# Sparse graph attention on one core: keys and values copied in one ScalarE operation, the key bias added by GpSimd, heavy batches summed by TensorE, distances first

## What is computed

```python
mask = adj + eye(n)
q = (h @ Wq.T + bq).reshape(n, 8, 32)        # k and v the same way
scores = einsum('nhd,mhd->hnm', q, k) / sqrt(32)
scores = where(mask == 0, -1e9, scores)
attn = softmax(scores, axis=-1)
ctx = einsum('hnm,mhd->nhd', attn, v).reshape(n, 256)
h1 = layer_norm(h + ctx @ Wo.T + bo)
out = layer_norm(h1 + relu(h1 @ W1.T + b1) @ W2.T + b2)
```

## Time and profile before

| | |
|---|---|
| median of three runs | 583.97 us (583.55 to 585.06) |
| profiled execution | 582.23 us |
| its span, first to last instruction | 580.4 us |
| mean granted TensorE clock | 0.952 of full speed |
| HBM traffic | 242 GB/s over the span |

### The profile page before, as it was taken

How to read it: one execution, slowest core, us unless ns; L and a number is a source line. 1 busy time by engine, 2 the same in 40 slices (tenths; PEclk the granted TensorE clock), 3 DMA queues, 4 the chain that set the end, 5 groups by cost and what they waited for, 6 DMA issues and landing times.

```text
span 580.4 us, 7599 instructions
## 1 busy us (share of the span) xinstructions
PE 500.2 (86%) x2434; PEld 399.7 (69%) x2434; DVE 452.5 (78%) x1066; ACT 181.5 (31%) x435; POOL 244.4 (42%) x366
## 2 busy tenths in 40 slices
PE   3999897875899999898898989969868888789994
PEld 2888796765568748755784776569545777469884
DVE  0788889998899999998999998786988998451103
ACT  0121142313432362252226124522522032432340
POOL 6111156433531576555654535414455536304133
PEclk9999999989799999997999999988978899789998
DMA  8999779998988699698769674425657823401011
GB/s 293 417 421 414 260 242 376 417 408 348 330 320 328 234 353 323 224 385 291 251 226 363 232 272 147 180 89 211 229 176 227 300 83 112 125 0 38 1 37 40
DMA packets 39227, 141.08 MB, mean 243 GB/s; under 512 B 4872, under 2 KB 15368, under 8 KB 35088
## 3 DMA queue, kind: packets, MB, share of 16 engines
q1 hardware_dynamic: 24336, 95.16, 43.9%
q0 software_dynamic: 13328, 43.55, 21.8%
q10 hardware_dynamic: 1520, 1.85, 0.9%
HBM read 123.74 MB, written 16.80 MB: 242 GB/s over the span
## 4 chain that ended last, share of the span: by engine, by line
PE 45%; DVE 35%; issue 9%; ACT 4%; DMA 3%; POOL 3%; POOLq 0%; another core or an unknown queue 0%; ACTq 0%; SPq 0%; DVEq 0%
DVE found L497 11%; PE ps L1031 10%; PE ps L1633 7%; PE ps L1044 7%; PE ps L1011 4%; PE ps L999 3%; PE ps L817 3%; PE ps L1651 2%; DVE stats L1098 2%; DMA work<-q_table,row_of 2%; DVE slots L663 2%; DVE slots L595 2%; DVE slots L676 2%; PE ps L818 2%; DVE work L547 1%
## 5 line engine op out<-in xcount | busy, mean ns | idle before, releaser
L497 DVE FIND_INDEX8 found<-ones,adj_buf 128x8 uint32<-128x4105 int32 (+5 forms) x40 | 138.7, 3467 | 0.0
L1031 PE MATMUL ps<-xT_all,w 128*128 128x512 f32 (+1 forms) x288 | 124.7, 581 | 0.2 <-ACT xT_all L1061 0.2
L1044 PE MATMUL ps<-w,xT_all 128*128 128x256 f32 x512 | 119.8, 388 | 2.6 <-ACT xT_all L1078 1.3
L1044 PEld LDWEIGHTS ps<-w,xT_all 128*128 128x128 f32 x512 | 97.1, 195 | 15.7 <-issue 1.6
L1031 PEld LDWEIGHTS ps<-xT_all,w 128*128 128x128 f32 x288 | 56.0, 203 | 46.4 <-issue 43.5
L959 POOL DMA_INDIRECT slots<-kv_table,col_of x54 | 56.8, 1051 | 40.5 <-DVE col_of L563 22.7
L1633 PE MATMUL ps<-early,xT_all 128*128 128x256 f32 x256 | 57.9, 388 | 9.4 <-DMA xT_all<-in_xT 9.4
L1078 ACT ACTIVATE xT_all<-ps,col_table 128x512 f32<-128x512 f32 (+1 forms) x72 | 45.8, 641 | 60.9 <-PE ps L1031 49.7
L1633 PEld LDWEIGHTS ps<-early,xT_all 128*128 128x128 f32 x256 | 49.6, 195 | 16.3 <-issue 9.3
L1098 DVE BATCH_NORM_STATS2 stats<-ps 128x6 f32<-128x256 f32 x62 | 22.2, 418 | 44.7 <-PE ps L999 44.7
L951 POOL DMA_INDIRECT slots<-kv_table,found x32 | 36.3, 1135 | 34.5 <-PE ps L818 14.8
(11 more groups left out here) (173 smaller groups left out, 860.3 us busy)
## 6 DMA issues: line engine op xcount, KB each, us to landing
adj_buf<-in_adj SPq DMA_DIRECT2D x31, 2048.0 KB
xT_all<-in_xT SPq DMA_DIRECT2D x15, 512.0 KB, 22.0
kv_table<-slots POOLq DMA_DIRECT2D x7, 1024.0 KB, 11.8
slots<-kv_table SPq DMA_DIRECT2D x12, 512.0 KB
q_table<-slots POOLq DMA_DIRECT2D x16, 256.0 KB, 10.1
out_dram<-early SPq DMA_DIRECT2D x7, 512.0 KB
q_own<-q_table SPq DMA_DIRECT2D x12, 256.0 KB
slots<-in_adj SPq DMA_DIRECT2D x1, 2048.0 KB, 24.9
```

Of the source, the lines that this page charges most:

```text
L497: last = nc.vector.max_index(dst, ones8[:], part)
L1031: last = nc.tensor.matmul(ps[:, q["bank"] + f % 2, 0:q["g"] * P], w1[:, k, f * P:(f + 1) * P], q["h1T"][:, k, :], start=(k == 0), stop=(k ...
L1044: nc.tensor.matmul(to, q["ffT"][:, f, j * P:(j + 1) * P], w2[:, f, :], start=(f == 0), stop=False)
```

## The change

- ScalarE takes keys and values of a pair out in one copy over both banks (`take_kv`, 128x1024). GpSimd adds the keys' bias in place in SBUF (`bias_k`) before its stores. VectorE has no part in the projection's output any more.
- The first load of x^T is cut in halves, the bias goes between them, and the three weight parts have a load and a semaphore each. TensorE waits for each where it first reads it.
- Tile 0's distances stand ahead of the last two table stores in ScalarE's order.
- In each step `distance_act` stands ahead of `dense(0)`; `mask_act` stays behind it. In a group of two steps feed-forward block 3 moves from gap 0 to gap 1.
- In batches 6 to 9 VectorE doesn't add the own slots; TensorE takes all three through the identity.
- Some semaphores are merged or dropped. The hunks that only declare them are left out below.

```diff
--- before.py
+++ after.py
@@ -61,6 +61,8 @@
         self.own = 1 + self.nu * self.A
         self.u0 = u0
         self.first = t == 0
+
+        self.adds = 0 if self.A == 2 else self.own - 1
         self.group, self.j = no // GROUP, no % GROUP
         self.rounds = [range(r, min(r + 4, self.U)) for r in range(0, self.U, 4)]
 
...
@@ -554,11 +555,11 @@
             nc.vector.tensor_scalar(row_of[q.par][:, 0:q.U], got[:, :, q.k + 1], -1.0 - (q.tiles[0] // 2) * 2 * P, 0.0, ALU.add, ALU.max)
             nc.vector.tensor_tensor(hot(q), slot_minus_edge[:, 0:q.k].unsqueeze(1).to_broadcast([P, q.U, q.k]),
                                     got[:, :, q.k:q.k + 1].to_broadcast([P, q.U, q.k]), ALU.is_equal).then_inc(hot_ready, 1)
-            dve.wait_ge(hot_ready, q.p + 1)
+            dve.wait_ge(hot_ready, 2 * q.p + 1)
             wait(dve, cols_ready, q.p)
             pick = picked[:, 0:q.U * q.k].rearrange("p (u k) -> p u k", k=q.k)
-            nc.vector.tensor_tensor(pick, hot(q), got[:, :, 0:q.k], ALU.mult).then_inc(picked_ready, 1)
-            dve.wait_ge(picked_ready, q.p + 1)
+            nc.vector.tensor_tensor(pick, hot(q), got[:, :, 0:q.k], ALU.mult).then_inc(hot_ready, 1)
+            dve.wait_ge(hot_ready, 2 * q.p + 2)
             with nc.allow_low_precision(reason="one whole number below 4096 and zeros"):
                 nc.vector.tensor_reduce(col_of[q.par][:, 0:q.U], pick, AX_X, ALU.add).then_inc(cols_ready, 1)
 
@@ -669,9 +670,9 @@
                     last = nc.vector.tensor_tensor(v[:, 1:], v[:, 1:], p.unsqueeze(3).to_broadcast([P, q.U, HEADS, DK]), ALU.mult)
             last.then_inc(own_weighted, 1)
             dve.wait_ge(own_weighted, q.b + 1)
-            done = total(lambda p: p.own - 1, q.b)
+            done = total(lambda p: p.adds, q.b)
             v = slots[q.par][:, 0:q.T * q.own, D:].rearrange("p (t s) d -> p t s d", s=q.own)
-            for a in range(1, q.own):
+            for a in range(1, 1 + q.adds):
                 wait(dve, own_sum, done + a - 1)
                 nc.vector.tensor_tensor(v[:, :, 0, :], v[:, :, 0, :], v[:, :, a, :], ALU.add).then_inc(own_sum, 1)
 
@@ -803,7 +804,8 @@
         def sum_pe(pe, q):
 
             pe.wait_ge(edge_weighted, q.b + 1)
-            wait(pe, own_sum, total(lambda p: p.own - 1, q.b + 1))
+            pe.wait_ge(own_weighted, q.b + 1)
+            wait(pe, own_sum, total(lambda p: p.adds, q.b + 1))
             pe.wait_ge(own_weighted, q.b + 1)
             wait(pe, ctx_ready, q.b)
             if q.b == SUM0:
@@ -815,7 +817,9 @@
                     for u in range(q.nu):
                         c = ti * q.nu + u
                         nc.tensor.matmul(to, edge_slots(q)[:, c, feats], onehot[q.par][:, c, :], start=(u == 0), stop=False)
-                    last = nc.tensor.matmul(to, own_slots(q, ti)[:, 0, feats], ident[:], start=False, stop=True)
+                    left = q.own - q.adds
+                    for a in range(left):
+                        last = nc.tensor.matmul(to, own_slots(q, ti)[:, a, feats], ident[:], start=False, stop=(a == left - 1))
             last.then_inc(acc_ps, 1)
 
 
@@ -1323,7 +1327,7 @@
 
         def ff_gap(place, count, gap):
             if count == 2:
-                return (((), (), (), (), (), (0, 1)), ((2, 3), (4,), (5, 6, 7), (), (), ()))[place][gap]
+                return (((), (), (), (), (), (0, 1)), ((2,), (3, 4), (5, 6, 7), (), (), ()))[place][gap]
             if count == 3:
                 return (((), (), (), (), (), (0, 1)), ((2,), (), (3, 4), (5,), (), ()), ((6,), (7,), (), (), (), ()))[place][gap]
             return (((), (), (), (), (), ()), ((0, 1), (), (2, 3), (4,), (), ()), ((5,), (), (6, 7), (), (), ()), ((),) * 6)[place][gap]
@@ -1351,8 +1355,13 @@
                 g = ORDER[c]
                 sp.dma_start(xT_all[:, c], xT_cols[:, :, g * GROUP * P:(g + 1) * GROUP * P]).then_inc(s_xT[c], 16)
 
-            sp.dma_start(bias_qk[:], bqkv[:, 0:2 * D].to_broadcast([P, 2 * D])).then_inc(s_bias, 16)
-            load_xT(0)
+
+            for half in range(2):
+                part = slice(half * 2 * P, (half + 1) * 2 * P)
+                sp.dma_start(xT_all[:, 0, :, part], xT_cols[:, :, ORDER[0] * GROUP * P:(ORDER[0] + 1) * GROUP * P][:, :, part]
+                             ).then_inc(s_xT[0] if half else s_first_xT, 16)
+                if half == 0:
+                    sp.dma_start(bias_qk[:], bqkv[:, 0:2 * D].to_broadcast([P, 2 * D])).then_inc(s_bias, 16)
             load_adj(sp, 0)
             load_xT(1)
             load_xT(2)
@@ -1449,11 +1458,23 @@
                 pool.wait_ge(s_q, i + 1)
                 pool.dma_start(q_tiles[i], q_stage[i % STAGES].rearrange("p (t d) -> p t d", d=D)).then_inc(s_q_out[i % STAGES], 16)
 
+            pool.wait_ge(s_bias, 16)
+
+            def bias_k(i):
+
+                c, r = 2 * i // GROUP, 2 * i % GROUP
+                k = kv_stage[c % STAGES][:, r:r + 2, 0:D]
+                pool.wait_ge(s_kv, i + 1)
+                nc.gpsimd.tensor_tensor(k, k, bias_qk[:, D:].unsqueeze(1).to_broadcast([P, 2, D]), ALU.add).then_inc(s_k, 1)
+
             for c in range(GROUPS - 1):
-                pool.wait_ge(s_k, (c + 1) * GROUP // 2)
-                pool.wait_ge(s_v, (c + 1) * GROUP // 2)
+                bias_k(2 * c)
+                bias_k(2 * c + 1)
+                pool.wait_ge(s_k, 2 * c + 2)
                 g = ORDER[c]
                 pool.dma_start(kv_tiles[:, g * GROUP:(g + 1) * GROUP, :], kv_stage[c % STAGES]).then_inc(s_kv_out[c % STAGES], 16)
+            bias_k(PAIRS - 2)
+            bias_k(PAIRS - 1)
             store_q(0)
             gather_aligned(pool, STEPS[0])
             gather_edges(pool, STEPS[0])
@@ -1513,18 +1534,20 @@
         @block.scalar
         def _(act):
             wqkv_rows = wqkvT.rearrange("(k p) n -> p k n", p=P)
-            act.dma_start(wqkv[:, :, D:], wqkv_rows[:, :, D:]).then_inc(s_first_weights, 16)
-            act.dma_start(wqkv[:, :, 0:D], wqkv_rows[:, :, 0:D]).then_inc(s_query_weights, 16)
+            for part in (1, 2, 0):
+                feats = slice(part * D, (part + 1) * D)
+                act.dma_start(wqkv[:, :, feats], wqkv_rows[:, :, feats]).then_inc(s_wqkv[part], 16)
             for dst, src in ((bias_qT, bq), (bias_kT, bk), (col_table, cols)):
                 act.dma_start(dst[:], src).then_inc(s_small, 16)
 
-            def take_v(i):
+            def take_kv(i):
                 c, r = 2 * i // GROUP, 2 * i % GROUP
                 act.wait_ge(s_kv_ps, i + 1)
                 if r == 0:
                     wait(act, s_kv_out[c % STAGES], c // STAGES * 16)
-                nc.scalar.copy(kv_stage[c % STAGES][:, r:r + 2, D:], ps[:, kv_bank(i, 1), :].rearrange("p (t d) -> p t d", d=D)
-                               ).then_inc(s_v, 1)
+                bank = kv_bank(i, 0)
+                nc.scalar.copy(kv_stage[c % STAGES][:, r:r + 2, :].rearrange("p t (b d) -> p b t d", d=D),
+                               ps[:, bank:bank + 2, :].rearrange("p b (t d) -> p b t d", d=D)).then_inc(s_kv, 1)
 
             def take_q(i):
                 act.wait_ge(s_q_ps, i + 1)
@@ -1537,20 +1560,19 @@
                 c, r = 2 * i // GROUP, 2 * i % GROUP
                 t = ORDER[c] * GROUP + r
                 act.wait_ge(s_k, i + 1)
-                act.wait_ge(s_v, i + 1)
                 act.dma_start(kv_tiles[:, t:t + 2, :], kv_stage[c % STAGES][:, r:r + 2, :]).then_inc(s_kv_last, 16)
 
             for i in range(PAIRS):
-                take_v(i)
+                take_kv(i)
                 if i == 6:
                     act.wait_ge(s_const, CONSTS)
                     distance_act(act, b0)
                     mask_act(act, b0)
                 if i == 13:
                     take_q(0)
-                if i >= PAIRS - 2:
-                    store_kv(i)
             distance_act(act, TILE0)
+            store_kv(PAIRS - 2)
+            store_kv(PAIRS - 1)
             mask_act(act, TILE0)
             for i in range(1, Q_BEFORE):
                 take_q(i)
@@ -1568,9 +1590,10 @@
                 if i == NB - 1:
                     post_act_x(act, JOBS[GROUPS - 1], GROUPS - 1)
                     post_act_x(act, JOBS[GROUPS], 0)
+                if i + 1 < NB:
+                    distance_act(act, STEPS[i + 1])
                 dense(0)
                 if i + 1 < NB:
-                    distance_act(act, STEPS[i + 1])
                     mask_act(act, STEPS[i + 1])
                 if place == 1 and n >= 1:
                     post_act_norm(act, JOBS[n - 1], n - 1, 1)
@@ -1618,17 +1641,18 @@
 
         @block.tensor
         def _(pe):
-            pe.wait_ge(s_first_weights, 16)
-
             def project_kv(i):
 
-                wait(pe, s_k, i - RING + 1)
-                wait(pe, s_v, i - RING + 1)
+                wait(pe, s_kv, i - RING + 1)
                 for j in range(2):
                     c, r = (2 * i + j) // GROUP, (2 * i + j) % GROUP
```

(22 more changed lines are left out.)

8 lines of the change are left out of this document (3 added, 5 removed).

## The result

The changed kernel takes 574.92 us, the median of four runs (573.47 to 577.28), beside 584.51 for the kernel before on the same chip (583.55 to 587.11). The ratio is 0.9859, with a 95% interval of 0.9813 to 0.9905: 1.41% of 583.97 is 8.2 us (5.5 to 10.9 by the interval), against 7.4 forecast; the two medians lie 9.6 us apart. The same kernel timed a second time, at the end of the experiments, gave 1.91%. The profiled execution took 575.76 us around a span of 574.0, against 582.23 around 580.4, so 6.4 us of the gain are there to be read.

A forecast was written before the change was run, and what follows sets the result against it. No engine alone was the bound: a chain alternates between TensorE and VectorE, VectorE leading slightly in heavy steps. Terms 2.0 + 1.8 + 3.6 = 7.4 us took the 584.0 median to 576.6, range 570.5 to 582.5.

The forecast's parts named there:

- Part 1: Projection start: smaller first loads let TensorE start 1.7 us earlier (1.2 to 2.9); 2.0 us together with Part 2.
- Part 2: Keys and values in the projection: VectorE loses 16 additions, step 0 starts 2.4 us sooner; 2.0 us together with Part 1.
- those 4.2 us: ScalarE's tile 0 distances, ahead of the last two table stores; stores issued at 73.9, first gather at 77.9.
- Part 3: Steps 6 to 9: TensorE gets 7.1 us more, VectorE 5.5 less; gain 1.8 us, ends -7.1 and 5.5.
- an earlier VectorE: Step 7: closes TensorE's 2.31 us idle gap for the one-hot rows, which lost some 2.3 us of clock.
- gather for addition: Rival that waits only move, here from an addition to a gather; 584.0 us, chance 0.06.
- become the bound: Rival for heavy steps 6 to 9: TensorE's added 7.1 us lie wholly on the path; 589.1 us, chance 0.08.
- Part 4: Steps 0, 1, 11, 14 and 17: VectorE waits less for ScalarE's distances; gain 3.6 us, ends 0 and 7.
- a new wait for the mask in 11 and 17: Sign of being right: in steps 11 and 17 VectorE would wait for the mask.
- All of it comes through: Rival: loads in time 3.5, heavy steps 5.5, distances 3.6, together 12.6 us; 571.4 us, chance 0.17.
- The tables did not come late: Denies the rival of late tables: start gains nothing, mask wait halves the distances' gain; 580.4 us, chance 0.17.
- GpSimd's additions did not block VectorE: Denies the rival that 16 projection additions each hold VectorE 1.27 us, 20.3 in all; 593.1 us, chance 0.03.

## Why the prediction was right, point by point

- **Part 1, the start: right.** The value weights landed at 7.82, forecast 7.7 to 8.2, and the projection ended 1.68 us sooner, forecast 1.7. "First projection near 7.6" was wrong by the letter: TensorE began at 4.77 and then stood for the value weights. Alone the part reaches step 0 and is gone by step 1.
- **Part 2: right in sum by luck, one step wrong, one missed.** Right: copies of 1.0 us, additions of 1.26, distances at 69.7 (69.3 forecast), a late adjacency tile costing up to 2 us (1.95 measured). Wrong: "the last two stores of the key/value table now stand behind those 4.2 us". They were issued at 70.71 and 71.18, not at 73.9, so the gather did not slip to 77.9, SP's wait for the gathers ended at 86.35 instead of 87.8, and step 0 could begin at 86.36. Missed: GpSimd's queue "holds nothing else there but the table stores" is false. The first query store (`store_q(0)`) is there, moved from 65.83 to 71.09, and the gather waits for it, 0.6 us longer than for ScalarE's stores. The sum came out because two sizes were off in opposite ways: step 0 came 3.89 us sooner where I had 2.4, and the late tile took 1.95 where I took off 0.4. With both, step 1 is 2.29 us sooner, where I took 2.0; the two parts timed alone sum to 0.51%, 3.0 us, with intervals of 1.9 us to either side for each.
- **Part 3, the sum: the step that failed is what gives it back.** Forecast: a gain of 1.8 us. Timed alone the part costs 1.6, give or take 1.9, so that a gain of 1.8 is excluded for it alone; on top of the rest it gains 1.1, which can't be told from nothing. The heavy stretch itself gained more than 1.8, by the means above 3.7 - 0.6 = 3.1 us, of which 1.4 is left at step 11. One term was no property of the kernel: the 2.3 us of clock that "an earlier VectorE" was to win back in step 7 is the bad luck of the one trace that I read. With the same idle time of 2.31 us and VectorE still adding, the kernel with the new start alone had the full level there. Two things had no term in the sum: the sum of step 9 runs on into step 10, which becomes 1.5 to 2.0 us longer, and VectorE, sooner at its edge product, waits for its gathers (0.90 and 2.73). I named "gather for addition" among the rivals as a wait that only moves, and gave it 0.06 for the whole kernel; for this part it is a good deal of the truth. TensorE was to be over 103 us busy in 226 to 336; it was 101.4 (98.4 in the earlier trace rows). It did not become the bound: in steps 6 to 9 it is busy for 98.03 of 105.88 us (93%), before for 96.86 of 108.45 (89%).
- **Part 4, distances first: the right mechanism, sized too small.** The term was 3.6 us; alone it measured 6.1, with 3.7 to 8.5 as its interval. By step: step 1 1.1 forecast, 1.25 measured; step 11 0.9 and 1.15; step 14 1.1 and 1.67; step 17 0.3 and 1.49. The last two carry most of the shortfall in that trace; by the means of all traces they are 0.8 and 0.9, and step 1, with 1.7, is the one that I had too low. I discounted step 14 by 0.45 for a mask that VectorE would still wait for, and took step 17 as blocked by feed-forward block 2. No wait for a mask appears in any trace, so "a new wait for the mask in 11 and 17" was wrong: the mask was ready whenever the distances were. In step 11 the next wait was for the lists (1.76), as written. Step 17's wait fell from 4.11 to 3.42, more than the 0.3, and a wait that I had not counted fell with it, that of step 18 for its gathers (1.96 to 0.54). Its gathers go out 0.7 us earlier in the step; the other 0.7 isn't explained, and the kernel with the new copies, which has no edit there, shows 1.00.
- **The rivals.** All of it comes through (571.4) is not what happened: of the heavy steps' 5.5 some 1.4 was left at step 11. The tables did not come late (first gather at 76.62), but the adjacency tile behind them did (1.95 us in the search at 95). GpSimd's additions did not block VectorE: the 40 searches total 138.7 us in both kernels, and the one at 69.07, with an addition at 69.88 beside it, took 4.43 us as in the earlier trace rows.
- The total was right because part 4 brought more and part 3 less than its term. That the two errors cancel is luck: timed alone the parts give 3.0, -1.6 and 6.1 where I had 2.0, 1.8 and 3.6. 8.2 measured against 7.4 is inside what the runs can tell; the second timing, 11.2 with 8.2 as its lower end, says that 7.4 was somewhat low. What the record can't support is a split of it to better than about 2 us a part.

## What to carry to other kernels

Where an engine's small operation gates others, put it ahead of the bulk work in its queue and look for the second queue that the same edit lengthens: here GpSimd's additions moved a store that nobody had listed. A stage with two engines near 90% busy gives up less than the work taken off one of them, and the other's extra work can surface in the stage behind it. And before a load is issued sooner, ask whose gathers it will share the DMA engines with.
